# Layer norms in front of a transformer stage moved into its first passes, constants set by GpSimd, and the weight loads released at the start of the block

## The reference, cut to what matters

```python
x = L0_attn_a_X                                    # (8, 512, 128) float32
x = x + _L0_attn_a_ref(_layernorm(x), ...)
x = x + _L0_ffn_ref(_layernorm(x), ...)
x = x + _L0_attn_b_ref(_layernorm(x), ...)         # the transformer stage
x = x + _L0_ffn_ref(_layernorm(x), ...)

def _layernorm(x, axis=-1, eps=1e-05):
    m = jnp.mean(x, axis=axis, keepdims=True)
    v = jnp.var(x, axis=axis, keepdims=True)
    return (x - m) / jnp.sqrt(v + eps)

def _forward(out, ...):                            # inside _L0_attn_b_ref
    for l in range(6):
        q, k, v = proj(Wq[l]), proj(Wk[l]), proj(Wv[l])      # with biases
        Qp, Kp = _favor_phi(q, omega[l]), _favor_phi(k, omega[l])
        a = _causal_linear_attention(Qp, Kp, v) @ Wo[l] + bo[l]
        h1 = _layer_norm(out + a, g1[l], be1[l])
        y = relu(h1 @ W1[l] + bf1[l]) @ W2[l] + bf2[l]
        out = _layer_norm(h1 + y, g2[l], be2[l])
    return out
```

## Time and profile before

| what | value |
|---|---|
| three runs | 3723.39, 3724.94 (median), 3729.19 us |
| the profiled execution, its own time | 3718.72 us |
| its span in the trace | 3717.0 us |
| busy over the span: PE, DVE, ACT, POOL | 92%, 72%, 45%, 24% |
| mean granted clock of TensorE | 0.976 of full speed |

### The profile page before, as it was taken

The page is one execution under the profiler, slowest core; times in us unless marked ns, Lnnn a source line. Parts: engine busy times, 40 slices in busy tenths (PEclk is TensorE's granted clock), DMA queues, the critical chain, the costliest instruction groups (busy, mean ns, idle before and its releaser), DMA issues. The chain is left out here.

```text
span 3717.0 us, 106102 instructions
## 1 busy us (share of the span) xinstructions
PE 3420.2 (92%) x43480; PEld 2611.4 (70%) x43480; DVE 2662.9 (72%) x6886; ACT 1684.2 (45%) x3438; POOL 901.7 (24%) x781
## 2 busy tenths in 40 slices
PE   4999999999999999799949999999999999977998
PEld 2777777777777777688836777767677777756887
DVE  3666666666666666688867888888788887857887
ACT  1555555555555555433324444444444444423332
POOL 3323332223323322100002223322332233320000
PEclk9999999999999999899979999999999999988999
DMA  2000000000000000000000000000000000000000
GB/s 89 28 27 28 25 28 28 24 30 26 28 27 28 24 24 24 7 1 0 0 15 17 3 17 3 3 17 3 17 3 3 17 3 3 3 2 1 1 1 23
DMA packets 38391, 60.20 MB, mean 16 GB/s; under 512 B 6960, under 2 KB 16688, under 8 KB 37552
## 3 DMA queue, kind: packets, MB, share of 16 engines
q1 hardware_dynamic: 37936, 53.78, 4.2%
HBM read 18.10 MB, written 2.10 MB: 5 GB/s over the span
## 5 line engine op out<-in xcount | busy, mean ns | idle before, releaser
L663 ACT ACTIVATE a_prob<-a_s,a_shift,a_scale 128x128 f32<-128x128 f32 (+3 forms) x512 | 312.2, 614 | 526.2 <-DVE a_shift L746 526.2
L1548 ACT ACTIVATE ffn_silu<-ffn_ps_g 128x512 f32<-128x512 f32 x272 | 161.3, 599 | 383.7 <-PE ffn_ps_g L1498 371.1
L1491 PEld LDWEIGHTS ffn_ps_y<-moe_down,ffn_hidden 128*128 128x128 f32 x2176 | 282.1, 191 | 41.5 <-issue 20.0
L1491 PE MATMUL ffn_ps_y<-moe_down,ffn_hidden 128*128 128x128 f32 x2176 | 288.1, 275 | 17.4 <-DVE ffn_acc L1652 17.4
L946 POOL TENSOR_TENSOR t_rstd<-t_var_eps,minus_half 128x4 f32<-128x4 f32 x96 | 97.6, 1017 | 792.0 <-DVE t_var_eps L1261 792.0
L1199 ACT COPY t_num<-t_n 128x512 f32<-128x512 f32 x96 | 56.3, 586 | 491.9 <-PE t_n L1007 491.4
L1652 DVE SCALAR_TENSOR_TENSOR ffn_acc<-ffn_ps_y,ffn_combine,ffn_acc 128x128 f32<-128x128 f32 x960 | 269.8, 345 | 7.5
L1664 DVE TENSOR_TENSOR ffn_hidden<-ffn_silu,ffn_ps_u 128x512 f32<-128x512 f32 x272 | 185.5, 684 | 108.7 <-ACT ffn_silu L1548 74.5
L1337 DVE TENSOR_TENSOR t_mixed<-t_s,upto 128x512 f32<-128x512 f32 x384 | 238.4, 684 | 15.7 <-PE t_s L983 13.8
L408 POOL TENSOR_TENSOR a_k_sin<-a_k_swap,sin_swap 128x512 f32<-128x512 f32 x64 | 81.4, 1272 | 669.9 <-DMA a_k_swap<-a_k_own 669.9
L983 PE MATMUL t_s<-t_phi_q,t_kz 32*128 32x64 f32 x6144 | 210.0, 277 | 31.1 <-DVE t_hid L1368 16.5
(11 more groups left out here) (210 smaller groups left out, 8501.1 us busy)
## 6 DMA issues: line engine op xcount, KB each, us to landing
a_k_swap<-a_k_own SPq DMA_DIRECT2D x128, 128.0 KB, 2.1
a_y_swap<-a_y_own SPq DMA_DIRECT2D x128, 128.0 KB, 2.0
a_staged<-in_pairs SPq DMA_DIRECT2D x8, 384.0 KB, 3.1
t_next<-in_t_w SPq DMA_DIRECT2D x12, 256.0 KB, 3.2
t_next_rows<-in_t_rows SPq DMA_DIRECT2D x6, 448.0 KB, 4.1
x<-in_x SPq DMA_DIRECT2D x8, 256.0 KB, 5.1
out<-x SPq DMA_DIRECT2D x1, 2048.0 KB, 8.7
t_next_sq<-in_t_sq SPq DMA_DIRECT2D x6, 256.0 KB, 2.7
```

The lines of the kernel that those rows point to most:

```text
L663: nc.scalar.activation(prob[c % 2][h][:, 0:(c + 1) * P], ps[f"s{h}"][:, 0:(c + 1) * P], ACT.Exp, bias=shift[:, k:k + 1], scale=scale[slot. ...
L1491: t = nc.tensor.matmul(ps_y[e % 2][:, c * P:(c + 1) * P], hidden[e % 3][:, c * P:(c + 1) * P], w_down[:, e * P:(e + 1) * P], start=True, s ...
```

## The change

The norm block ahead of the transformer block goes. Inside the transformer block each group is normalised in two parts on VectorE: `first_part(g)` (statistics and `var_eps`) and `second_part(g)` (writes `o`, gives `normed`), with GpSimd's `power(g)` between. Groups 0 and 1, and the first part of group 2, stand ahead of the pipeline; in slots LEAD to z = 4 VectorE does `second_part(in+2)` and `first_part(in+3)` behind its step S1, and GpSimd `power(in+3)` in its own S1. ScalarE's `turn` waits for `normed` in layer 0. The memsets move from VectorE to GpSimd, the copy to `omega` stays on VectorE, and VectorE gives its two semaphores to SyncE as its first act.

```diff
--- before.py
+++ after.py
@@ transformer_block, declarations
+        own = [v_pad[SPAN * p:SPAN * (p + 1), :, :, p, :].rearrange("p (c s) k n -> p c s k n", s=2) for p in range(2)]
...
@@ GpSimd
+                def power(g):
+                    pool.wait_ge(first_eps, g + 1)
+                    nc.gpsimd.tensor_tensor(first["rstd"][:], first["var_eps"][:], mem["minus_half"][:, 0:TILES],
+                                            ALU.pow).then_inc(first_rstd, 1)
+
                 def body(step, slot, sequence):
+                    if step == "S1" and slot.of("in") + 3 < B:
+                        power(slot.of("in") + 3)
...
                 begin(pool, "o_bias rstd scaled h1b o_new")
+                flat = v_tok[:].rearrange("p c s h d -> p c s (h d)")
+                nc.gpsimd.memset(flat[:, :, 1, :], 1.0).then_inc(ones_set, 1)
+                power(0)
+                nc.gpsimd.memset(v_pad[:].rearrange("p u k h n -> p (u k h n)"), 0.0).then_inc(ones_set, 1)
+                nc.gpsimd.memset(kv[:].rearrange("p u h n -> p (u h n)"), 0.0).then_inc(ones_set, 1)
+                power(1)
+                pool.wait_ge(ones_set, 3)
+                pool.wait_ge(first_rstd, 2)
+                pool.nop(nofuse=True)
+                nc.gpsimd.memset(flat[0:SPAN, :, 0, :], 1.0).then_inc(ones_set, 1)
+                pool.wait_ge(ones_set, 4)
+                nc.gpsimd.memset(flat[SPAN:P, :, 0, :], 0.0).then_inc(ones_set, 1)
+                for p in range(2):
+                    for span in range(2):
+                        pool.wait_ge(ones_set, 5 + 2 * p + span)
+                        nc.gpsimd.memset(own[p][:, :, span, :, D:V], 1.0).then_inc(ones_set, 1)
+                pool.wait_ge(ones_set, 9)
+                power(2)
                 pipeline(pool, plan, weights_in, weights_out, body)
@@ ScalarE
                     if slot is None:
-                        act.wait_ge(ones_set, 10)
+                        act.wait_ge(omega_set, 1)
...
                     if step == "turn":
-                        act.wait_ge(s["o_new"], slot.of("in") + 2)
+                        if slot.of("in") < B:
+                            act.wait_ge(normed, slot.of("in") + 1)
+                        else:
+                            act.wait_ge(s["o_new"], slot.of("in") + 2)
@@ VectorE
-                flat = v_tok[:].rearrange("p c s h d -> p c s (h d)")
-                nc.vector.memset(flat[:, :, 1, :], 1.0).then_inc(ones_set, 1)
-                nc.vector.memset(flat[0:SPAN, :, 0, :], 1.0).then_inc(ones_set, 1)
-                nc.vector.memset(flat[SPAN:P, :, 0, :], 0.0).then_inc(ones_set, 1)
-                nc.vector.memset(v_pad[:].rearrange("p u k h n -> p (u k h n)"), 0.0).then_inc(ones_set, 1)
-                nc.vector.memset(kv[:].rearrange("p u h n -> p (u h n)"), 0.0).then_inc(ones_set, 1)
-                nc.vector.tensor_copy(omega[64:P, :], mem["half_norm"][64:P, :]).then_inc(ones_set, 1)
-                dve.wait_ge(ones_set, 6)
...
-                        nc.vector.memset(own[p][:, :, span, :, D:V], 1.0).then_inc(ones_set, 1)
-                dve.wait_ge(ones_set, 10)
+                dve.sem_inc(made_in["dve"], 1)
+                dve.sem_inc(made_out["dve"], 1)
+
+                def first_part(g):
+
+                    for c in range(TILES):
+                        nc.vector.bn_stats(first["stats"][:, c, :], mem["x"][:, (g * TILES + c) * P:(g * TILES + c + 1) * P]
+                                           ).then_inc(first_stats, 1)
+                    dve.wait_ge(first_stats, (g + 1) * TILES)
+                    dve.nop(nofuse=True)
+                    for c in range(TILES):
+                        nc.vector.bn_aggr(first["mean_var"][:, c, :], first["stats"][:, c, :]).then_inc(first_mv, 1)
+                    dve.wait_ge(first_mv, (g + 1) * TILES)
+                    nc.vector.tensor_scalar(first["var_eps"][:], first["mean_var"][:, :, 1], LN_EPS, None,
+                                            ALU.add).then_inc(first_eps, 1)
+
+                def second_part(g):
+
+                    dve.wait_ge(first_rstd, g + 1)
+                    dve.nop(nofuse=True)
+                    for c in range(TILES):
+                        at = slice((g * TILES + c) * P, (g * TILES + c + 1) * P)
+                        t = nc.vector.tensor_scalar(mem["o"][:, at], mem["x"][:, at], first["mean_var"][:, c, 0:1],
+                                                    first["rstd"][:, c:c + 1], ALU.subtract, ALU.mult)
+                    t.then_inc(normed, 1)
+
+                first_part(0)
+                nc.vector.tensor_copy(omega[64:P, :], mem["half_norm"][64:P, :]).then_inc(omega_set, 1)
+                second_part(0)
+                first_part(1)
+                second_part(1)
+                first_part(2)
+                dve.wait_ge(ones_set, 9)
...
+                        if t_ == 1 and slot.of("in") + 2 < B:
+                            second_part(slot.of("in") + 2)
+                        if t_ == 1 and slot.of("in") + 3 < B:
+                            first_part(slot.of("in") + 3)
...
-                dve.sem_inc(made_in["dve"], 1)
-                dve.sem_inc(made_out["dve"], 1)
@@ build
-                norm_block(nc, mem, B, attention=False, tag=tag)
                 transformer_block(nc, mem, ins, B)
```

More of the change, by code:

```diff
@@ L869, in transformer_block @@
         made_out = {n: sem("made_out_" + n) for n in ("act", "dve", "pool")}
-        ones_set = sem("ones_set")
+        ones_set, omega_set = sem("ones_set"), sem("omega_set")
+        first = {"stats": sb("first_stats", [P, TILES, 6]), "mean_var": sb("first_mean_var", [P, TILES, 2]),
+                 "var_eps": sb("first_var_eps", [P, TILES]), "rstd": sb("first_rstd", [P, TILES])}
+        first_stats, first_mv, first_eps = sem("first_stats"), sem("first_mv"), sem("first_eps")
+        first_rstd, normed = sem("first_rstd"), sem("normed")
         LOADS = 6
```

## The result

The change takes 3705.57 us (median of five runs, 3701.21 to 3708.65) against 3723.39 us for the kernel before (five runs, 3720.04 to 3729.19): ratio 0.995 with a 95% interval of 0.9935 to 0.9964, that is 17.8 us less. The forecast was 3706.0 and 18.9 us less. The profiled execution took 3706.51 us, its span is 3704.7 us.

What follows compares the result with a forecast made beforehand. At the seam before the first projection a serial chain, not TensorE, was taken as the bound. Terms: −25.4 (start) + 6.3 (three seams) + 0.2 (FIRST to z = 1) = −18.9 us, giving 3706.0 against the median; range 3695 to 3716.

Steps and rivals of the forecast that it cites:

- The serial chain: Ahead of the first projection: norms, memsets and weight loads run one after another though none needs all before; gain 25.4 us.
- LEAD and FIRST: First slots of layer 0: added norm work at LEAD to FIRST costs nothing, covered by 1.85 us of idle time.
- The start, its terms: Block start: load issue after about 0.5 us, loads 7.15, then norms, memsets and bv; projection at 1893.5 instead of 1918.88.
- The blocking: Block start: VectorE's second part of group 0 runs behind GpSimd's v_pad memset, on a shared port lock; gain 25.4, without it 27.1.
- The memset rate: GpSimd memsets at block start: 1.195 ns an element, taken from its plain copy; another rate would be a sign of being wrong.
- The rival without it: Block start: no lock between memset and VectorE, gain 20.6 us, total 3704; chance 0.15.
- The seams: Layer 0, slots z = 1, 2 and 3 to the next: TensorE waits 2.1 us at each, 6.3 us in all.
- 3 us either way for the clock: LEAD and FIRST: allowance for where TensorE's half-speed stretches fall among the matmuls; no gain forecast from the clock.
- The slots did not hide the norms: Rival, layer 0 slots: VectorE's 4.5 us of room hides all norm work; gain 25 to 27 us, 3698 to 3700; chance 0.15.
- the memsets did not set the start: Rival, block start: GpSimd memsets at 2.49 ns an element put the projection near 1898; gain 14.5 us, 3710; chance 0.10.
- not every seam cost in full: Rival, layer 0: no slack takes anything, five seams cost 4.8 us each, 24 in all, total 3723; chance 0.08.
- slots z = 2 to 4 kept the full clock: Rival: new 2 us stalls drop TensorE to 1.2 GHz in these slots, costing 41 us, total 3747; chance 0.03.

Runs made afterwards that it cites:

- the loads alone: Kernel before, with VectorE freeing the weight loads ahead of its memsets instead of behind them: 3717.25 against 3726.43 us, ratio 0.9975.
- the repeated series: The unaltered changed kernel timed once more, beside the version with both edits: 3701.25 against 3721.61 us for the kernel before, ratio 0.9941.
- the memset that waits: Changed kernel with GpSimd's two long memsets starting only after the second part of group 0: one execution, 3713.12 us.
- the experiment without norms: Changed kernel without the norms of groups 2 to 7, layer 0 reading x instead: 3694.91 against 3726.43 us, ratio 0.9916.
- both edits: Changed kernel with first part moved behind the Wo statistics, its pow behind h1b, and bv copied before group 1's second part: ratio 0.9935, repeated 0.9919.

## Why the prediction was right

- **The serial chain** was the step with the most weight, and it held: 25.1 us measured at the projection, 25.4 forecast. The experiment with the loads alone gives the share of one link, 6.9 us.
- **The total** was hit more closely than its terms. Up to the start of slot z = 5 the traces give 25.1 − 6.4 − 1.8 = 16.9 us (the 1.8 in LEAD and FIRST, below), 2 less than the forecast 18.9. The medians say 17.8 us, those of the repeated series 20.4, and the executions of one kernel spread over 7 us and more. That the two medians of the result agree with the forecast to 1.1 us is partly luck.
- **The start, its terms.** The load's issue (0.70 us instead of 0.5) and its length (7.90 instead of 7.15; 6.8 to 7.9 in the other kernels) were a little short. The projection came at 13.71 us against 13.4 by errors that cancel: the chain up to `bv` was 0.8 us shorter than forecast, and a wait of 1.07 us behind it was not forecast. The memsets run at 0.88 ns an element (1.80 us for 2048), not at the 1.195 of the copy row; the estimate from the Trainium skill (GPSIMD Engine Reference, Elementwise — side-by-side cycle accounting), 0.86, was the better one. The blocking was stronger than forecast, 2.7 us instead of 2.3, and of another order: the forecast let VectorE in between the two long memsets and made `pow` of group 1 wait for the second. In fact VectorE waited through both, and `pow` then waited 2.20 us for VectorE. The memset rate, which the forecast called a sign of being wrong, was wrong; its error and that of the blocking offset each other in part. And the last 1.07 us ahead of `bv` were in no term; the row puts them down to issue, and 0.97 to 1.17 us of idle time stand ahead of `bv` in all other versions with norms in the slots. Their cause is open.
- **The blocking** that the forecast took from the `kz` row is shown by the memset that waits: 3.83 and 1.11 us for the same instructions. The rival without it falls; its total (3704) would have fitted the result as well as the forecast did, so only the rows decide.
- **The seams.** 6.4 us measured, 6.3 forecast, and the experiment without norms takes back 5.5. Inside a seam the sizes were off: the second part hardly waited for GpSimd's adds (1.17 to 1.39 us instead of about 1.6), so the residual was 2.65 us late at the first of them and not 3.1. The 0.2 us put at the seam into z = 1 did not show (28.17 us instead of 28.14).
- **LEAD and FIRST** were forecast at nothing, with 3 us either way for the clock, and lost 3.3 us. 1.5 of it is the wait for `bv`, which counts in the start already. The other 1.8 us are not the norms: both edits leave the norms in these two slots as they are, and there the slots are 27.62 and 29.49 us long (27.58 and 29.44 the first time), as before (27.67 and 29.42). They fit the clock: in the change the first scores of FIRST took 3.94 us instead of 2.31 and its projection 3.57 instead of 1.98. The windows of slot FIRST in the profile of the change, in a second execution of the same kernel, and in the version with both edits:

```profile
1922.12:1953.78 31.66, 24.59 (x530) 18.51 (x529) 17.36 (x47) 10.51 (x18) 1.01 (x1) 0.82 0.01 3
```

```profile
1922.16:1956.53 34.37, 29.50 (x533) 22.82 (x533) 17.34 (x47) 10.50 (x18) 1.01 (x1) 0.65 0.01 2
```

```profile
1915.21:1944.70 29.49, 23.83 (x533) 18.59 (x529) 17.25 (x47) 10.52 (x18) 1.41 (x2) 0.83 0.01 3
```

The first two are the same kernel, and the slot is 31.66 us at a mean clock of 0.82 and 34.37 at 0.65. The third does the same work in 29.49 at 0.83, as the kernel before did (29.42). At nearly the same mean, the place of the half-speed stretch makes 2 us. The first 8 us of the slot in the change and with both edits:

```profile
1922.12:1930.12 8.00, 7.33 (x66) 5.24 (x66) 4.84 (x17) 2.15 (x4) 0.00 (x0) 0.50 0.01 2
```

```profile
1915.21:1923.21 8.00, 6.22 (x79) 4.29 (x76) 6.03 (x19) 4.90 (x8) 1.01 (x1) 1.00 0.01 2
```

The change does the projection at 1.2 GHz (0.50), the other at 2.4 GHz; its half-speed stretch comes later, at 0.53 from 1931.21 to 1939.21. The forecast allowed 3 us for the clock; in the second execution LEAD and FIRST together are 7.5 us longer than before, of which 2.4 are the wait for `bv`, so the allowance was too small. What decides the place of the stretch stays open.

- **The rivals.** The slots did not hide the norms, the memsets did not set the start, though by little (they end at 1895.08, VectorE's norms at 1895.84, and without the first part of group 2 only 0.29 us are won), not every seam cost in full, and slots z = 2 to 4 kept the full clock with TensorE idle for 2.2 to 3.6 us in each.

## What to carry to other kernels

A serial setup between two stages is worth its full length, so ask of each piece what it really needs; here only one of eight groups and one load of weights. Work that moves into a busy pipeline is paid for by its place: the same 1.5 us of VectorE cost 2 us a slot ahead of an engine that waits, and next to nothing where VectorE waited for another engine anyway. And whatever moves to GpSimd should not run beside a `tensor_scalar` of VectorE from SBUF to SBUF on the path that sets the end (here 3.83 us instead of 1.11 beside memsets, 2.11 and 2.37 instead of 1.17 beside an add).

## What the runs showed of the hardware

A short stretch of TensorE at 1.2 GHz falls into steady slots in which TensorE is busy almost throughout, without any change there. In the kernel with the loads alone, whose slots are those of before, slot z = 2 has it and the next one not:

```profile
1996.18:2026.42 30.24, 28.78 (x551) 21.61 (x552) 23.23 (x63) 12.76 (x22) 8.38 (x8) 0.94 0.01 3
2026.42:2054.40 27.98, 26.96 (x538) 20.15 (x536) 23.08 (x63) 12.66 (x22) 8.38 (x8) 1.00 0.01 2
```

A mean clock of 0.94 over 30.24 us comes to an estimated 3.6 us at half speed, and the slot is 2.3 us longer than the next. Which slots have such a stretch differs from execution to execution (with both edits it was z = 2 the first time and z = 5 the second), so a gain of 2 us in one slot shows in the trace only where the clock column stands beside it. The first two stages are the same in all kernels, and yet the first norm instruction behind them came between 1877.9 and 1884.0 us.
